# Gated delta-rule attention on one core: head 1 with its two batches exchanged, four-corner 64x64 products, and a state update of four operations on VectorE

## What is computed

```python
attn = -(k_beta @ k.T * decay_mask), strictly lower; attn = inverse by rows, + eye
value_corrected = attn @ v_beta
k_cumdecay = attn @ (k_beta * g_exp)
def chunk_step(state, c):
    intra = where(mask_upper1, 0, (q_c @ k_c.T) * dm_c)
    v_prime = v_c - kcd_c @ state
    inter = (q_c @ state) * ge_c
    out = inter + intra @ v_prime
    new_state = state * gel_c + (k_c * kd_c).T @ v_prime
```

## Time and profile before

| | us |
|---|---|
| median of 3 executions | 4982.58 |
| lowest and highest | 4973.11, 4985.07 |
| the profiled execution | 4975.11 |
| its span in the trace | 4973.3 |
| PE busy | 4647.1 |
| DVE busy | 3576.1 |
| ACT busy | 3061.3 |
| POOL busy | 1089.0 |

### The profile page before, as it was taken

The page is one execution under the profiler, slowest core; times in us unless marked ns, Lnnn a source line. Parts: engine busy times, 40 slices in busy tenths (PEclk is TensorE's granted clock), DMA queues, the critical chain, the costliest instruction groups (busy, mean ns, idle before and its releaser), DMA issues.

```text
span 4973.3 us, 144942 instructions
## 1 busy us (share of the span) xinstructions
PE 4647.1 (93%) x54288; PEld 3181.4 (64%) x54320; DVE 3576.1 (72%) x6424; ACT 3061.3 (62%) x7979; POOL 1089.0 (22%) x1064
## 2 busy tenths in 40 slices
PE   4998899999999899999999899999999899999998
PEld 2555666666666566666666566666666666666666
DVE  7554677777777577777777677777777677777775
ACT  2333666666666566666666566666666566666665
POOL 0000122222222122222222122222222222222222
PEclk8999999999999999999999999999999999999999
DMA  2111222222223222222223222222223322222221
GB/s 61 37 38 62 65 68 55 60 66 61 66 58 75 65 68 51 62 67 61 66 52 80 69 55 60 66 61 67 55 60 82 69 58 59 64 66 61 68 55 37
DMA packets 760109, 305.29 MB, mean 61 GB/s; under 512 B 672880, under 2 KB 716016, under 8 KB 749168
## 3 DMA queue, kind: packets, MB, share of 16 engines
q1 hardware_dynamic: 620144, 287.40, 23.4%
q10 hardware_dynamic: 139264, 8.42, 1.8%
HBM read 216.96 MB, written 66.07 MB: 57 GB/s over the span
## 4 chain that ended last, share of the span: by engine, by line
PE 74%; issue 9%; DVE 8%; DMA 3%; SPq 3%; ACT 2%; POOL 1%; DVEq 0%; ACTq 0%; POOLq 0%
PE pj L661 18%; PE dsb L820 8%; PE pj L656 7%; PE dsb L792 5%; PE pot L778 5%; PE pod L804 5%; PE ms L694 4%; PE pot L749 4%; PE pod L761 3%; PE ms L674 3%; PE pj L651 2%; PE ms L688 2%; PE pot L606 2%; DVE cy L1293 2%; PE dsb L811 2%
## 5 line engine op out<-in xcount | busy, mean ns | idle before, releaser
L1293 DVE SCALAR_TENSOR_TENSOR cy<-xpad,cw,cy 128x1024 f32<-128x1024 f32 x768 | 1104.9, 1445 | 7.4 <-ACT cy L1004 0.4
L661 PE MATMUL pj<-xnT,wt 128*128 128x512 f32 x2048 | 1020.3, 621 | 33.6 <-DMA cw<-in_L_attn_conv_weight 20.0
L1563 POOL TENSOR_TENSOR rout<-rin,expo 128x2 f32<-128x2 f32 x512 | 358.3, 700 | 2205.0 <-DVE rin L1438 2176.1
L1557 POOL TENSOR_TENSOR sdec<-st,gel 128x512 f32<-128x512 f32 x384 | 402.3, 1048 | 1156.5 <-DVE st L1427 953.9
L820 PE MATMUL dsb<-wo,yT 128*128 128x256 f32 x2048 | 574.8, 403 | 13.5 <-issue 12.4
L661 PEld LDWEIGHTS pj<-xnT,wt 128*128 128x128 f32 x2048 | 352.1, 191 | 362.9 <-issue 348.1
L1003 ACT ACTIVATE xpad<-pj 128x512 f32<-128x512 f32 x512 | 305.0, 596 | 358.9 <-PE pj L661 358.5
L656 PE MATMUL pj<-wt,xnT 128*128 128x256 f32 x2048 | 509.9, 392 | 0.0
L1063 ACT ACTIVATE yT<-dsb 128x256 f32<-128x256 f32 x512 | 202.2, 395 | 483.3 <-PE dsb L811 480.5
L1427 DVE TENSOR_TENSOR st<-dsb,sdec 128x512 f32<-128x512 f32 x384 | 265.3, 691 | 324.0 <-PE dsb L792 324.0
L820 PEld LDWEIGHTS dsb<-wo,yT 128*128 128x128 f32 x2048 | 348.2, 190 | 118.5 <-issue 90.4
(11 more groups left out here) (175 smaller groups left out, 8336.8 us busy)
## 6 DMA issues: line engine op xcount, KB each, us to landing
qge<-ge_rows SPq DMA_DIRECT2D x64, 1024.0 KB, 7.4
wt<-in_L_attn_W_qkvz SPq DMA_DIRECT2D x64, 768.0 KB, 4.9
gb<-g_rows SPq DMA_DIRECT2D x128, 256.0 KB
a_d<-at SPq DMA_DIRECT2D x64, 512.0 KB, 2.6
wo<-in_L_attn_W_out SPq DMA_DIRECT2D x64, 256.0 KB, 2.7
x_d<-xpair SPq DMA_DIRECT2D x128, 128.0 KB, 1.7
ap_<-a_d SPq DMA_DIRECT2D x512, 16.0 KB, 1.8
dd<-x_d SPq DMA_DIRECT2D x512, 16.0 KB, 1.9
```

Of the source, the lines that this page charges most:

```text
L661: last = mm(pj[n % 2][:, :], wt[:, k, col:col + DH], batch(xnT, k, i), start=(k == 0), stop=(k == KD - 1))
L1293: stt(y, x[:, :, tap:tap + SEQ], cw[:, kind, tap:tap + 1], y, ALU.mult, ALU.add).then_inc(S["conv"], 1)
L1557: tt(sdec[:, :, :, :], st[:, c % 2, :, :, :], bc(gel[:, p, :, :].rearrange("p h (b c) -> p b h c", b=NB)[:, :, :, c], 3, DH), ALU.mult).th ...
L1563: tt(rout[:, :], rin[:, :], expo[:, 0, 0:GRP], ALU.pow).then_inc(S["routs"], 1)
```

## The change

For value head 1 the two batches change places in everything that lies by token rows: the triangles stay, but what a product reads from partitions 0 to 63 it writes to 64 to 127. `home(b, h)` says where. `solve` and `intra` then have four products on four different corners: head 0 on (0, 0) and (64, 64), head 1 on (0, 64) and (64, 0). The loops over batch and head change places, so that neighbours in the order differ in their corner. Head 1's outputs lie exchanged: `key_state` and `query_state` take them by batch and head (`key_state` in four products of 128 columns instead of two of 256), the z projection makes head 1's half in two column halves of the array, and `out_project` is one whole-array product for head 0 and two column-half products for head 1, which put the rows back. Four PSUM banks are one tensor `quad` with new places for the core's results. The z product has 12 calls an entry instead of 4.

Units are numbered by head and then chunk. `kn`, `kn2` and `qe` have a second, exchanged copy for head 1, which costs two small operations each on DVE (64 partitions by 8), and the power for `kn` takes 16 elements a partition instead of 8. The vt entries are copied by four ACT instructions of 128 columns instead of two of 256. POOL's `decay_state` and `sdec` are gone; `update_state` computes state times factor plus increment in four operations of 128x128, for each batch and head. The wait of the first intra for `og` moves ahead of chunk 0's `out_project`, the last intra waits for `accs` too, the second half of a fixpoint round takes the turned form in all rounds, the first round waits for the third ACT negation too, and the wait for the DMA `eturn` moves from PE to DVE.

```diff
+        quad = ctx.enter_context(nc.psum_tensor("quad", [P, 4, 512], F32))
+        pot, pod, pch, pds = (quad[:, n, :] for n in range(4))
+        po = quad[:, 0:2, DH:2 * DH]
+        pod_rows = quad[:, 0, 2 * DH:2 * DH + D]
+        pw = quad[:, 1:3, 0:DH]
+        pks = quad[:, 2, 0:GRP * DH]
+        pyt = quad[:, 3, 0:GRP * DH]
+        pstate = quad[:, 2:4, GRP * DH:2 * GRP * DH]
...
+        def home(b, h):
+
+            return b if h == 0 else 1 - b
...
                         c = 2 * i + v
+                        dst = pj[n % 2][:, v * GRP * DH:(v + 1) * GRP * DH]
                         for k in range(KD):
-                            last = mm(pj[n % 2][:, v * GRP * DH:(v + 1) * GRP * DH], xnT[:, k, c * P:(c + 1) * P],
-                                      wt[:, k, 4 * DH:4 * DH + GRP * DH], start=(k == 0), stop=(k == KD - 1))
+                            mm(dst[:, 0:DH], xnT[:, k, c * P:(c + 1) * P], wt[:, k, 4 * DH:5 * DH],
+                               start=(k == 0), stop=(k == KD - 1))
+                        for k in range(KD):
+                            for b in range(NB):
+                                last = mm(dst[half(b), DH:], xnT[:, k, c * P + (1 - b) * CH:c * P + (2 - b) * CH],
+                                          wt[:, k, 5 * DH:6 * DH], start=(k == 0), stop=(k == KD - 1),
+                                          tile_position=(0, b * CH))
...
             def key_state(g, p, c):
                 after(pe, "ss_", g, c)
                 apart(pe)
-                for b in range(NB):
-                    last = mm(pkw[half(b), 0:GRP * DH], kq[:, p, c, b, :],
-                              st[:, c % 2, b, :, :].rearrange("p h d -> p (h d)"), start=True, stop=True,
-                              tile_position=(0, b * CH))
+                for h in range(GRP):
+                    for b in range(NB):
+                        last = mm(pks[half(b), h * DH:(h + 1) * DH], kq[:, p, c, home(b, h), :],
+                                  st[:, c % 2, home(b, h), h, :], start=True, stop=True, tile_position=(0, b * CH))
...
                 apart(pe)
-                for h in range(GRP):
-                    for b in range(NB):
-                        rhs = rr[half(b), h, :] if c else vb[p][half(b), h, :]
-                        last = mm(pkw[half(b), (GRP + h) * DH:(GRP + h + 1) * DH], bda[half(b), p, c * GRP + h, :],
-                                  rhs, start=True, stop=True, tile_position=(b * CH, b * CH))
+                for a in range(NB):
+                    for h in range(GRP):
+                        rhs = rr[half(a), h, :] if c else vb[p][half(a), h * NC, :]
+                        last = mm(pw[half(home(a, h)), h, :], bda[half(a), p, h * NC + c, :], rhs,
+                                  start=(c == 0 or h == 1), stop=True, skip_group_check=True,
+                                  tile_position=(a * CH, home(a, h) * CH))
                 last.then_inc(S["wp"], 1)
...
             def intra(g, p, c):
-                if c == 0:
-                    before(pe, "og", g)
                 if c == NC - 1:
                     after(pe, "wev", g, NC)
+                    after(pe, "accs", g, c - 3 + 1)
                 apart(pe)
-                for h in range(GRP):
-                    for b in range(NB):
-                        last = mm(po[half(b), h * DH:(h + 1) * DH], it[half(b), p, c * GRP + h, :], ww[half(b), h, :],
-                                  start=(c == 0), stop=True, skip_group_check=True, tile_position=(b * CH, b * CH))
+                for b in range(NB):
+                    for h in range(GRP):
+                        last = mm(po[half(home(b, h)), h, :], it[half(b), p, h * NC + c, :], ww[half(b), h, :],
+                                  start=(c == 0), stop=True, skip_group_check=True,
+                                  tile_position=(b * CH, home(b, h) * CH))
                 last.then_inc(S["op"], 1)
 
             def output_rows(g, p, j):
...
-                    last = tp(dsb[:, 1, (GRP + h) * DH:(GRP + h + 1) * DH], zz[p][:, j, h, :], ident)
+                    last = tp(pyt[:, h * DH:(h + 1) * DH], zz[p][:, j, h, :], ident)
                 last.then_inc(S["yt"], 1)
...
-            def out_project(g, p, j):
+            def out_project(g, p, j, bank_cleared):
                 if j == 0:
                     after(pe, "wos", g, 1)
                 after(pe, "yte", g, j + 1)
                 all_but_last(pe, "accs", g, j)
-                for h in range(GRP):
-                    last = mm(dsb[:, 0, GRP * DH:GRP * DH + D], yT[:, h, :], wo[:, p, h, :],
-                              start=(h == 0), stop=(h == GRP - 1))
+                mm(pod_rows, yT[:, 0, :], wo[:, p, 0, :], start=not bank_cleared, stop=False, skip_group_check=True)
+                for b in range(NB):
+                    last = mm(pod_rows[half(b)], yT[:, 1, half(1 - b)], wo[:, p, 1, :], start=False, stop=True,
+                              skip_group_check=True, tile_position=(0, b * CH))
                 last.then_inc(S["od"], 1)
 
             def front_piece(g, hk, s):
...
                 if c:
                     key_state(g, p, c)
                     query_state(g, p, c)
+                else:
+                    before(pe, "og", g)
                 two, three = behind(g, p, c, 2, first), behind(g, p, c, 3, first)
                 if three:
-                    out_project(*three)
+                    out_project(*three, c > 0)
                 if two:
                     output_rows(*two)
...
-                    for v in range(2):
-                        c = 2 * i + v
-                        last = fn(vb[p][:, c * GRP:(c + 1) * GRP, :].rearrange("p h d -> p (h d)"),
-                                  src[:, v * GRP * DH:(v + 1) * GRP * DH], ACT.Copy, scale=kn[:, c:c + 1])
+                    for v in range(4):
+                        c, h = 2 * i + v // GRP, v % GRP
+                        last = fn(vb[p][:, h * NC + c, :], src[:, v * P:(v + 1) * P], ACT.Copy, scale=kn[:, h, c:c + 1])
...
             def update_state(g, p, c):
                 after(dve, "ds", g, c + 1)
-                src = dsb[:, :, 0:GRP * DH]
+                src = pstate
                 dst = st[:, (c + 1) % 2, :, :, :].rearrange("p b h d -> p b (h d)")
                 if c:
-                    after(dve, "sdecs", g, c)
-                    tt(dst, src, sdec[:, :, :, :].rearrange("p b h d -> p b (h d)"), ALU.add).then_inc(S["ss_"], 1)
+                    if c == 1:
+                        loaded(dve, d_ge, g, 1)
+                    for b in range(NB):
+                        for h in range(GRP):
+                            last = stt(st[:, (c + 1) % 2, b, h, :], st[:, c % 2, b, h, :],
+                                       gel[:, p, h, b * NC + c:b * NC + c + 1], pstate[:, b, h * DH:(h + 1) * DH],
+                                       ALU.mult, ALU.add)
+                    last.then_inc(S["ss_"], 1)
                 else:
                     dve.tensor_copy(dst, src).then_inc(S["ss_"], 1)
 
...
-            def decay_state(g, p, c):
-                if c == 1:
-                    loaded(pool, d_ge, g, 1)
-                    apart(pool)
-                after(pool, "ss_", g, c)
-                tt(sdec[:, :, :, :], st[:, c % 2, :, :, :],
-                   bc(gel[:, p, :, :].rearrange("p h (b c) -> p b h c", b=NB)[:, :, :, c], 3, DH), ALU.mult
-                   ).then_inc(S["sdecs"], 1)
```

114 lines of the change are left out of this document (55 added, 59 removed).

## The result

| | us |
|---|---|
| before, median of 4 executions | 4983.82 (4973.11 to 4990.67) |
| after, median of 4 executions | 5069.40 (5062.74 to 5075.96) |
| ratio, 95% interval | 1.0172 (1.0156 to 1.0188) |
| span of the profiled execution | 4973.3 before, 5060.9 after |

The account below looks back on a forecast made before the run. PE's blocks in program order were taken to bound the kernel. PE's own +0.88, shrinking waits -0.68 and growing waits +1.13 gave +1.33 us a head, x 64 = +85 us: about 5065 us, forecast's own range 5015 to 5110.

Parts of the forecast that it names:

- The rival of two abreast: In solve and intra the four corners run only two at a time, no gain: 5287 us, 3%.
- Part 1: Solve and intra blocks on PE: four corners take 0.37 us instead of 0.58, -3.47 us a head.
- Part 2: Undoing the exchange on PE by changes of tile size: out_project +2.80 us a head, z entries +1.55.
- The fourth rival: Detours at out_project and z cost half, as weights for column halves load ahead: 4928 us, 7%.
- Part 3: State update on DVE: 1.12 us for 0.69, six times a head, hidden by PE; without POOL's work DVE comes out level.
- Waits that shrink: PE's waits for DVE L1340 (-0.4), for rr (-0.18) and for the eturn DMA (-0.1): -0.68 us a head.
- Waits that grow: PE's new or longer waits for ACT, at vt entries, ww and square sums: +1.13 us a head.
- (c) and (d): Square sums of chunks 1 and 3 wait longer for ACT behind the shorter intra: +0.22 us a head each.
- (a): The last vt entry's transposes wait for a bank that ACT empties with four copies an entry: +0.47 us a head.
- (b): At chunk 7 PE waits longer for ACT's ww, so the solve's gain is lost: +0.22 us a head.
- The third rival: The new waits of PE don't form, as ACT is early enough: 4983 us, no change, 13%.
- DVE as the bound: Each +0.43 us of the state update reaches PE and POOL's absence returns nothing: 5230 us, 4%.

Follow-up runs that it names:

- z_plain: Changed kernel with z made as one whole-array product, so head 1's gate meets swapped rows; out_project keeps its halves: 5057.31 us.
- two_corners: Changed kernel with head 1's solve and intra products sent to head 0's two corners, all detours kept: 5161.08 us.
- out_plain: Changed kernel with head 1's out_project as one whole-array product, its rows left swapped; z keeps its halves: 4979.77 us.
- both_plain: Changed kernel with z and out_project both as whole-array products, so the exchange is not undone: 4984.63 us.
- vt_two: Changed kernel with vt entries emptied by two ACT copies of 256 columns instead of four of 128: 5070.76 us.
- state_alone: Kernel before with only the four-operation update_state on DVE and POOL's decay_state gone: 4957.69 us.
- after_light: Changed kernel with the last of a convolution's three DVE products cut from 512 columns a sequence to 8: 5064.60 us.
- gate_back: Changed kernel with head 1's rows put back by DVE's product with the gate; z and out_project whole-array, whole computation kept: 5124.44 us.
- rows_swapped: Changed kernel with head 1's transpose written in exchanged halves and out_project whole-array; z keeps its halves, whole computation kept: 4974.74 us.

## Why the prediction was right, point by point

**The time is the sum of PE's blocks in program order: right as a sum, too simple as a reason.** Forecast 5065, measured 5069. The forecast gave all of it to the woven heads, 1.33 x 64 = 85 us. Measured are 1.15 x 63 = 72.5 us there, 2.8 ahead of them and 12.3 in the last head. Two errors, of -12 and of +15 us, nearly cancel, and that the number came out within 4 us is luck.

**Part 1, four corners: right.** 0.20 us less a block, 0.217 forecast; 3.2 us a head for 3.47. The rival of two abreast is out by the rows of 0.38 us. Those rows also have both row tiles writing one PSUM bank. The Trainium skill, TensorEngine Tiling (Array Packing), Restrictions and Gotchas, says that different row tiles cannot access the same PSUM bank simultaneously; in this kernel, with each tile in its own partitions, the trace doesn't agree: 8 records of 128 columns in 0.38 us are four abreast.

**Part 2, the detours: sizes right, place wrong.** out_project 0.29 us a block for 0.35; z 0.44 for 0.35 at three entries, 0.54 for 0.50 at the fourth. PE's own sum of these and part 1 is about +1.0 us a head by blocks, +0.88 forecast. By the windows view PE is busy 1.16 us more a head, of which the lower granted clock makes 0.16. out_project's detour is what makes the kernel slower than before: without it the time is 4980 us, and 4975 with the whole computation kept. That each detour lies on the path was the wrong step. z_plain gets back 12 us of the 88 that PE saves there; waits for DVE, DMA, ACT and issue take the rest, 0.64, 0.21, 0.23 and 0.41 us a head. two_corners shows the same of part 1's gain. The fourth rival, faster by half-price detours, decided below 0.24 us a detour: they cost more, and it is out.

**Part 3, the state update: right.** 1.12 us as forecast, the pairs of 3.28 us are gone (L1305's mean is 1282 ns for 1445), DVE comes out level. By itself the part gains 25 us; the prediction had this only as a share of its shrinking waits.

**Waits that shrink: -0.68 forecast, -0.73 measured,** by the releasers DVE and DMA (0.94 to 0.40, 0.52 to 0.33). L1340's is gone, 0.54 a head for the 0.4 forecast. The waits for rr that part 3 was to take away did vanish, and were larger than the list of waits showed: 0.44 us a head at the solves of chunks 1, 3 and 6, for the 0.18 forecast. But the listed wait grew from 11.5 to 18.8 us, since a second one opened at chunk 7: output_rows to solve is 0.73 us there on the mean, 0.37 at the other chunks. The step that failed took all of the listed wait for the work of the slowed L1293 pairs; the earlier PE is, the longer it waits for rr (42.3 us in out_plain, 78.4 in both_plain).

**Waits that grow: +1.13 forecast, +0.72 measured** (ACT 0.34 to 0.82, issue 1.17 to 1.41). (c) and (d), the square sums of chunks 1 and 3, were +0.44; measured (37.6 - 10.6) / 64 = +0.42. (a), the vt copies, was +0.47; vt_two shows 0, and PE waits 1.3 us for them in the whole kernel. The step that failed took PE's arrival at the fourth entry from before, without looking at what stands ahead of it: the last fixpoint round now waits for DVE's L1425. The list has 7.2 us, 30 times, for 1.5 us, once; with the shorter ones the round starts 1.26 us behind the first entry for 1.02 before (medians), 0.15 behind the end of L1425. (b), ww at chunk 7, was +0.22; it fell, from 10.7 us to 4.3, and no run isolates why. The growth of issue, +0.24, was in no term. The third rival, no new waits, is half right: two of its four did not form. Its 4983 us is out all the same, by PE's own sum and the last head.

**The last head: missed.** It has no front to fill PE's waits, so DVE's longer update (6 x 0.43 = 2.6 us) and out_project's detours (8 x 0.29 = 2.3) lie open there. state_alone takes 51.1 us, just the 2.6 above before. two_corners, with the detours as well, takes 55.0 at a granted clock of 0.99; after, with the corners' gain, 60.8 at 0.84. But this head varies: in after_light, whose edit doesn't reach it, the same instructions take 56.4 us at 0.91, and in vt_two 60.8 at 0.84 again. So the corners' gain gave nothing back in this head and cost 1 to 6 us there, and some 4 of the 12.3 us are what the clock did in the one execution that was profiled.

**DVE as the bound: 4% were too few for what stood behind it.** As written, each +0.43 reaching PE, it is out. But DVE's 52 of 68.6 us was given against it, an average over a head. In its 16 full us DVE is the co-bound of before too, and this, with the waits for code, and not PE's price list, is why undoing z's detours pays so little. How the two share it is not shown.

## What to carry to other kernels

An engine that is 72% busy over the span can be full for a quarter of every round; before PE time is priced, ask the windows of each stage which engine has no idle time in front of any row, and where the program joins it. Time saved ahead of such a join comes back in part or nearly whole as a wait, time saved behind it is kept. Moving work of the full engine into its own idle time ahead of the stretch (two lines, 37 us) gave three times what z's detours gave back (12 us for 1.4 us of PE a head). Waits of the same cause can be too short for a list of waits: 0.44 us a head showed only in the distances of starts. When a wait for one engine is removed and the time stays, read who is named next at the same instruction: two chains may end there together.

## What the runs showed of the hardware

- Idle time on PE is paid twice when the clock falls behind it. In gate_back waits of 1.09 and 0.97 us were followed by 3.41 us at a granted clock of 0.50, where 32 products took 1.91 us in the place of 1.06. In the last head the granted clock is 0.84 in after, and 0.99 in two_corners, which has the same program but for the corners. The windows view of two_corners, to set beside the two above:

```profile
5090.60:5145.60 55.00, 37.90 (x374) 23.54 (x374) 22.00 (x69) 18.09 (x72) 6.26 (x9) 0.99 0.09 20
```

  The eleven kernels with four-corner blocks have 0.78 to 0.93 in this head, the three with two corners (before, state_alone, two_corners) 0.97 to 1.00. What in the four-corner blocks brings it down no run isolates, and after_light's 0.91 beside the 0.84 of after, for the same instructions, shows how far one execution can be from another.
- A wait of PE that the profile puts down to nothing is mostly one for code: 448 of 482 such waits of over 0.8 us end 1.2 to 1.8 us behind a 16 KB transfer of kind "instruction". In the woven heads all issue waits together are 74 us in before, 89 in after and 115 in z_plain.
- A PE transpose that writes its 128 columns to PSUM in two exchanged halves costs what a plain one does (rows_swapped against out_plain: 4975 and 4980 us, and 0.31 us from output_rows to solve in both).
